# Two tiles' small matmuls in one burst: an attention-and-norm kernel reordered by pairs of tiles

## The reference, cut to what matters

```
x = L0_attn_x                              # (8, 2048, 512) float32
x = x + _layernorm(attn(_layernorm(x)))
x = x + _layernorm(ffn(_layernorm(x)))

# attn: Q, K, V = h @ W.T + b, reshaped (n, s, 16, 32) and transposed to (n, 16, s, 32)
scores = einsum('nqhd,nkhd->nhqk', Q, K) / sqrt(32)
out = einsum('nhql,nlhd->nqhd', softmax(scores), V).reshape(n, s, e) @ Wo.T + bo

# ffn: s_len, bsz, d_model = x.shape; cap = s_len // n_head
y = t + outs                               # outs: top_k(scores, cap) tokens alone
yn = (y - mean) * rsqrt(var + 1e-5) * ln_g + ln_b
```

## Time and profile before

| | us |
|---|---|
| median of 3 runs | 1691.34 |
| lowest, highest | 1689.78, 1692.69 |
| span of the profiled execution | 1686.3 |
| PE busy in it | 1657.2 (98%) |
| DVE busy | 1309.6 (78%) |
| POOL busy | 1285.2 (76%) |
| ACT busy, without its DMA issues | 855.4 (51%) |

### The profile page before, as it was taken

The page is one execution under the profiler, slowest core; times in us unless marked ns, Lnnn a source line. Parts: engine busy times, 40 slices in busy tenths (PEclk is TensorE's granted clock), DMA queues, the critical chain, the costliest instruction groups (busy, mean ns, idle before and its releaser), DMA issues.

```text
span 1686.3 us, 55468 instructions
## 1 busy us (share of the span) xinstructions
PE 1657.2 (98%) x22550; PEld 1320.8 (78%) x22550; DVE 1309.6 (78%) x2455; ACT 855.4 (51%) x1730; POOL 1285.2 (76%) x1303
## 2 busy tenths in 40 slices
PE   8999999999999999999999999999999999999994
PEld 6777887877878778788877877887887887787873
DVE  7687877877877877778778778778787787787777
ACT  4355455555544544554555555445445555555453
POOL 5577877877877778778778778787787787787777
PEclk9999999999999999999999999999999999999997
DMA  7666666666666666666666666666666676666553
GB/s 252 173 172 184 176 169 171 182 178 174 166 188 170 175 175 183 172 179 179 172 170 179 180 175 166 184 175 171 173 186 170 173 187 171 173 168 189 155 139 88
DMA packets 388635, 293.46 MB, mean 174 GB/s; under 512 B 296854, under 2 KB 296854, under 8 KB 388380
## 3 DMA queue, kind: packets, MB, share of 16 engines
q1 hardware_dynamic: 345552, 223.02, 49.8%
q10 hardware_dynamic: 42828, 66.90, 13.2%
HBM read 155.46 MB, written 67.24 MB: 132 GB/s over the span
## 4 chain that ended last, share of the span: by engine, by line
PE 95%; DVE 2%; issue 1%; ACT 1%; POOL 1%; ACTq 1%; DMA 0%; DVEq 0%
PE ps_k L1080 8%; PE ps_y L1160 7%; PE ps_y L1161 7%; PE ps_v L1080 7%; PE ps_y L1164 7%; PE ps_v L1083 7%; PE ps_v L1081 7%; PE ps_q L1080 7%; PE ps_k L1081 7%; PE ps_q L1083 7%; PE ps_k L1083 7%; PE ps_q L1081 7%; PE ps_s L1121 6%; PE ps_o L1140 5%; ACTq L943 0%
## 5 line engine op out<-in xcount | busy, mean ns | idle before, releaser
L910 ACT ACTIVATE q_sb<-ps_q,mr 128x512 f32<-128x512 f32 x127 | 87.5, 689 | 537.6 <-issue 537.6
L403 POOL TENSOR_TENSOR z<-z,b_row 128x512 f32<-128x512 f32 x124 | 187.5, 1533 | 222.7 <-DVE z L679 222.7
L605 DVE STREAM_TRANSPOSE qT<-q_sb 128x512 f32<-128x512 f32 x128 | 137.6, 1075 | 107.4 <-ACT q_sb L910 106.9
L1080 PE MATMUL ps_k<-wk_hi,xT_hi 128*128 128x512 f32 x504 | 212.2, 421 | 0.3 <-issue 0.3
L1160 PE MATMUL ps_y<-wo_hi,oT_hi 128*128 128x512 f32 x504 | 200.3, 397 | 2.1 <-ACT oT_hi L926 1.9
L1161 PE MATMUL ps_y<-wo_lo,oT_hi 128*128 128x512 f32 x504 | 199.7, 396 | 0.0
L1080 PE MATMUL ps_q<-wq_hi,xT_hi 128*128 128x512 f32 x504 | 199.5, 396 | 0.0
L1081 PE MATMUL ps_k<-wk_lo,xT_hi 128*128 128x512 f32 x504 | 199.2, 395 | 0.4 <-issue 0.4
L1080 PE MATMUL ps_v<-wv_hi,xT_hi 128*128 128x512 f32 x504 | 199.4, 396 | 0.0
L383 POOL TENSOR_TENSOR x_t<-x_t,mr_row 128x512 f32<-128x512 f32 x126 | 195.7, 1553 | 4.4 <-ACT mr_row L1005 4.4
L1081 PE MATMUL ps_q<-wq_lo,xT_hi 128*128 128x512 f32 x504 | 198.9, 395 | 0.0
(11 more groups left out here) (189 smaller groups left out, 3721.0 us busy)
## 6 DMA issues: line engine op xcount, KB each, us to landing
x_in<-in_xa SPq DMA_DIRECT2D x64, 512.0 KB, 4.9
x_t<-in_xt SPq DMA_DIRECT2D x64, 512.0 KB, 4.8
k_bd<-kT SPq DMA_DIRECT2D x512, 64.0 KB, 2.4
v_d<-v_tok ACTq DMA_DIRECT2D x128, 256.0 KB, 2.2
v_key<-v_d SPq DMA_DIRECT2D x128, 256.0 KB, 3.9
res<-in_xr SPq DMA_DIRECT2D x64, 512.0 KB, 4.9
p_bd<-pT ACTq DMA_DIRECT2D x508, 64.0 KB, 2.3
out<-o_sb SPq DMA_DIRECT2D x62, 512.0 KB, 2.9
```

The costliest lines, as they stand in the source:

```text
L403: nc.gpsimd.tensor_tensor(z[:, j, :], z[:, j, :], b_row[:, :], ALU.add).then_inc(z_done, 1)
L605: nc.vector.transpose(qT[t % 2][:, :, :].rearrange("p n h -> p h n"), q_sb[:, :].rearrange("p (h d) -> p h d", d=D)).then_inc(qT_done, 1)
L1080: nc.tensor.matmul(ps, x_hi[:, e, :], w_hi[:, e, :], start=e == 0, stop=False)
```

## The change

PE's loop is now over pairs p = 2 to 62: scores of two tiles, mixings of two tiles, then the eight dense products of two tiles with the outputs between them. For this `ps_s` and `ps_o` hold two tiles side by side (`half_of`), `top` and `total` have two buffers and `z` two pairs. `less_top` waits for both tiles' scores, `o_high` and `o_low` for both tiles' mixings. Mixing and output of a tile come one turn later: tile a's scores stand in pair p + 1, its mixing and output in pair p + 2. All other engines have loops over pairs too, with their steps in another order. The opening and the ending are written anew: which engine does which `end_*` step, and which PSUM bank takes which of the last outputs.

```diff
-            for s in range(4, NT - 2):
-                scores(s - 1)
-                mixed(s - 2)
-                keys(s)
-                queries(s)
-                values(s)
-                output(s - 2)
+            for p in range(2, NV - 1):
+                a, b = 2 * p, 2 * p + 1
+                scores(a - 2)
+                scores(b - 2)
+                mixed(a - 4)
+                mixed(b - 4)
+                keys(a)
+                queries(a)
+                values(a)
+                keys(b)
+                output(a - 4)
+                queries(b)
+                values(b)
+                output(b - 4)
+            scores(NT - 4)
             scores(NT - 3)
-            mixed(NT - 4)
+            mixed(NT - 6)
+            mixed(NT - 5)
             keys(NT - 2)
             queries(NT - 2)
             values(NT - 2)
             keys(NT - 1)
+            queries(NT - 1)
+            output(NT - 6)
             scores(NT - 2)
+            scores(NT - 1)
+            mixed(NT - 4)
             mixed(NT - 3)
-            queries(NT - 1)
+            values(NT - 1)
+            output(NT - 5)
             output(NT - 4)
-            scores(NT - 1)
-            values(NT - 1)
+            output(NT - 3)
             mixed(NT - 2)
-            output(NT - 3)
+            mixed(NT - 1)
             output(NT - 2)
-            mixed(NT - 1)
             output(NT - 1)
```

```diff
+        def half_of(t):
+            return slice(E // 2 * (t % 2), E // 2 * (t % 2) + E // 2)
+
+        def both(t):
+            return (t | 1) + 1
+
+        def mixed_in(t):
+            return ps_s[:, :, half_of(0)] if t == NT - 1 else ps_o[:, :, half_of(t)]
+
+        def mixed_by(t):
+            return NT - 1 if t == NT - 2 else both(t)
```

Of the ending, the last steps of ACT, as an instance:

```diff
+            probs_half_out(NT - 2)
+            y_scaled(NV - 3)
+            probs_half_out(NT - 1)
             o_high(NT - 2)
-            end_turn("A", END, 1, x1_of(END), x1_of(END))
-            z_scaled(NV - 3)
-            probs_half_out(NT - 1)
-            end_turn("B", END, 2, end_z_of[0], x1_of(END))
+            end_turn("A", END)
+            end_turn("A", END + 1)
+            o_high(NT - 1)
```

More of the change, by code:

```diff
@@ L354, in _ @@
             probs_half_out(NT - 1)
+            sp.wait_ge(x1_done, 2 * (NV - 2))
+            load_r(NV - 1)
+            end_store(END + 1)
+            end_store(END)
             store(NV - 3)
[L356 to L357 removed]
+            end_store(END + 2)
+            end_store(END + 3)
             for i in range(2):
@@ L475, in _ @@
             x_centre(5)
-            for s in range(4, NT - 2):
-                v = (s - 4) // 2
-                if s % 2 == 0 and pair(v):
-                    root("A", v)
[L481 to L493, removed]
-                    root("B", v, 1.0 + EPS, EPS * EPS)
-                    if v == 0:
-                        pool.wait_ge(b_loaded, 3 * DMA)
-                    for j in range(2):
[L498 to L508, removed]
-                    for j in range(2):
-                        out_add(v, j)
@@ new lines, in _ @@
+            z_add(NV - 5, 0)
+            z_add(NV - 5, 1)
+            x_low(NT - 1)
+            root("A", NV - 4)
+            normalise(NT - 4)
+            pool.wait_ge(r_loaded[(NV - 4) % 2], DMA * ((NV - 4) // 2 + 1))
+            x1_add(NV - 4, 0)
+            x1_add(NV - 4, 1)
+            root("C", NV - 5)
+            normalise(NT - 3)
+            root("B", NV - 4, 1.0 + EPS, EPS * EPS)
+            z_scale(NV - 4, 0)
+            z_scale(NV - 4, 1)
+            root("C", NV - 4)
+            out_add(NV - 4, 0)
@@ L1045, in _ @@
-            x1_scaled(NV - 3)
+            cast("o", 0, wo_hi)
+            x_high(5)
+            cast("o", 1, wo_hi)
+            for p in range(2, NV - 1):
+                a, b = 2 * p, 2 * p + 1
+                v, u = p - 3, p - 4
+                o_high(a - 4)
+                o_high(b - 4)
+                exponent(a - 2)
+                exponent(b - 2)
+                if pair(v):
+                    y_scaled(v)
+                q_in(a)
+                v_in(a)
+                x_high(a + 2)
+                probs_out(a - 2)
+                probs_out(b - 2)
+                if pair(v):
+                    x1_scaled(v)
+                q_in(b)
+                if pair(u):
+                    z_scaled(u)
+                v_in(b)
+                x_high(b + 2)
```

517 lines of the change are left out of this document (300 added, 217 removed).

## The result

The changed kernel takes 1826.2 us (median of 4 runs, 1824.7 to 1830.5), the one before 1691.0 (1689.8 to 1692.7): a ratio of 1.080 [1.079, 1.082]. 1667.0 had been forecast, with a range up to 1677. The profiled execution has a span of 1822.9 us, where the sum of the prediction had 1662.0. So 161 us are to be found.

The account below looks back on a forecast made before the run. PE was taken to bound the kernel. From a span of 1686.3 us, 21.8 (bursts), 1.9 (opening) and 0.6 (ending) came off, giving 1662.0; plus 5.0 outside the span, 1667.0 us, range 1662 to 1677.

Parts of the forecast that it names:

- What bounds the kernel: Whole kernel: PE, busy 98% of the span, sets the time; other engines matter only where PE waits.
- list of three ways: Time can be won only if PE does less or the same faster, the opening waits less, or the ending shortens.
- The burst, 0.33 us for its ends, 21.8 us: Rows of small matmuls on PE: each costs 0.33 us for entry and exit; 66 fewer bursts save 21.8 us.
- The second runs as fast as the first: PE's burst: a second block of 64 small matmuls takes 0.65 us against 0.66, 10 ns a matmul.
- Rival 3: Long bursts on PE run slower: added blocks at twice their 0.65 us give 1746 us, far more by the skill's page; chance 0.03.
- Stalls in the loop, 0: PE's loop over pairs: no waits for other engines, 0 us taken.
- the slacks at SP, ACT, POOL: Loop: spare time before PE would wait: SP's odd-tile keys 2.7 us, ACT 1.7 and 3, POOL's step 2.2.
- rival 1: The loop's order leaves PE waiting 0.1 to 0.35 us a pair: 1673 to 1688 us, likeliest about 1676; chance 0.14.
- rival 2: Odd tile's keys come late on SP, four DMAs behind `rows_store`: slower, 1728 us if `x_root` ends at 22.1; chance 0.04.
- The opening, 0.5 us of waits: Ahead of the loop and in its first turns: PE waits 0.5 us instead of 2.4, gaining 1.9 us.
- The ending, 64.1 us: From the burst of scores 124 and 125 to the end: 64.1 us against 64.7, gaining 0.6 us.
- The sum: Span 1686.3 - 21.8 - 1.9 - 0.6 = 1662.0 us; with 5.0 above the span, 1667.0 us.

Follow-up runs that it names:

- run 9: Changed kernel, 56 idle instructions a pair in mid-pair, 76 ahead of the loop, 100 in the ending, tile 3's keys before two loads, ending reordered: 1676.5 us, ratio 0.9921.
- run 6: Changed kernel, 56 idle instructions a pair (7 behind each dense product), 76 ahead of the loop, tile 3's key DMAs issued before two 512 KB loads: 1691.1 us.
- run 8: Changed kernel, 56 idle instructions a pair one by one, 71 ahead of the loop, 100 in the ending, tile 3's keys before loads, ending reordered: 1690.0 us, ratio 0.9989.
- run 5: Kernel before, with each tile's scores computed twice (tiles 4 to 124), giving bursts of 192 matmuls, 384 instructions: 1949.6 us.

## Why the prediction was wrong, point by point

- **What bounds the kernel** (PE, and others only where PE waits): right in the engine, but the list of three ways to win or lose time left one out, that PE is given no instructions. The page of before had the counts for it, x22550 and the packets of its instruction queue, and I didn't weigh them.
- **The burst, 0.33 us for its ends, 21.8 us**: right. Pairs without a pause take 25.33 against 25.37, and cutting the burst in two costs 0.35 (25.68 - 25.33). The Trainium skill, "TensorEngine Tiling (Array Packing)", "Key Properties", has a drain at each change of mode; the 0.33 us at a burst's ends fits that and would be its size for one way in and out; that it is a drain no run shows.
- **"The second runs as fast as the first", so four blocks cost 4 x 0.65**: the step that failed. For each matmul it holds (1.51 us for 128 scores and 1.31 to the next, in every kernel); for the instructions that bring them it doesn't. Rival 3, "long bursts run slower", was the right place with a wrong mechanism: it asked for slower matmuls at a fixed pace, 1746 us or far more, and the runs show matmuls at full pace with one pause at a border of 256 instructions: the burst took 4.67 us on average and not 2.73, and with what the clock adds 2.38 us a pair are lost. It had been given 0.03 because rows of two blocks spoke against a slower pace; those rows could say nothing on a burst with two borders well inside it, because a burst of before has 256 instructions and not 512. I had said that they "can't speak for 256", and gave this no weight in the chances or the range.
- **Stalls in the loop, 0; the slacks at SP, ACT, POOL; rivals 1 and 2**: right, as far as the runs tell. In run 9, whose loop has the new order unchanged and most pairs at 25.33, PE waits for their data in the loop's first pair and later once, for 0.1 us.
- **The opening, 0.5 us of waits**: the place was right (scores(3) at keys), the size was wrong. Keys were said to land at 50.3, from 2.4 us of landing in the loop; the stretch behind 1 MB of loads has 7.4, PE waits 5.3 us there, and the row of the page is a median over 512 DMAs. With a pause on top the first pair took 34.6 us and not 25.4. Put ahead of the loads, the keys cost 0.8 to 1.1 us of waiting (runs 6 and 9).
- **The ending, 64.1 us**: 72.4. PE's part came out near, and partly by luck: from the burst at 1750.51 the last dense group starts at 1795.87, and its slot ends 46.3 us after the burst, where 45.5 had been walked. But 3.2 us of that are pauses that nobody forecast, the wait at mixed(127) was 1.5 and not 2.8, and the 1.7 us of slower clock behind it didn't come (clock 1.00, last group at 0.234 us a matmul). What was mis-sized is the tail: 26.1 us from there to the end instead of 18.6. The chain that ended last runs through POOL from 1786.8, 10 us before PE's last slot ends, to 1814.1, with no gap above 0.25 us: POOL does ten additions and scalings of tiles 122 to 125 there, 13.2 us, and the last tiles' roots take their turn among them. That another order would give back all 7.5 us isn't shown: runs 8 and 9, which put the last tiles' steps first, have tails of 25.8 and 25.4.

```profile
1750.51 1.51 PE L1241 MATMUL ps_s<-k_bd,qT 64*32 64x64 f32 x128
...
1790.33 0.85 PE L1263 MATMUL ps_s<-p_bd,v_key 64*32 64x64 f32 x64 [1.48 <-issue]
...
1795.87 1.09 PE L1289 MATMUL ps_v<-wo_hi,oT_lo 128*128 128x512 f32 x4
...
1819.72 0.75 DVE L803 SCALAR_TENSOR_TENSOR x_in<-x_in,end_rsC,x 128x512 f32<-128x512 f32 x1 [0.51 <-POOL end_rsC L450]
```

- **The sum**: with the pauses away it comes close. Run 9's span is 1674.8 against the 1662.0 forecast; the rest is 0.9 in the start of the loop, 1.8 in the first pair, 60 x 0.07 = 4 in the loop and 6 in the ending.

What stays open: why the packet for a burst starts 1 us ahead of it in one place and 1 to 2 us behind its start in another a few instructions away. The place without pauses was read off the changed kernel's trace and tried, not worked out. Whether the packets come so slowly because the core's other DMAs are under way (their share is 0.65 in the loop) no run tests.

## What to carry to other kernels

Count an engine's instructions, not only its work: wherever a row of short ones is longer than a block of 256 (here 128 small matmuls, each with its weight load), price each further block of 256 by the time between two packets of the instruction queue (3.3 to 4.4 us in nine of ten of the changed kernel's paused bursts) and not by the matmuls. If such a burst can't be cut, make a loop's turn a whole number of blocks with instructions that do nothing, keep those away from the burst's edges, and try where the border falls. And for DMAs take the landing time of the stretch, with the loads ahead of it, not the median of the page.

## What the hardware showed that had not been expected

- PE's instructions come in packets of 16 KB, 256 instructions: 45,620 in 178 packets here, and 61,110 in 238 in run 5. Two starts are never less than 3.28 us apart. The Trainium skill, "Runtime: NRT & Kernel Launch", "Instruction fetch mechanics", has the blocks of 256, and the count agrees; it says of their fetching that it is hidden by the pace at which instructions are issued. That doesn't hold for matmuls of 10 ns, as the pauses of 1.5 to 3 us show.
- Idle instructions of PE are free in dense code up to 14 in a row, and 50 in a row cost 0.3 to 0.8 us.
- A pause of about 2 us in PE's work was followed in about a quarter of the pairs by some 3.5 us at the lower clock level (1.2 GHz), which cost 1.55 us more. Why not in the others wasn't found.
